# Halving normalized tokens before they are turned, turning them by DMA, and unrolling the experts of an attention and mixture-of-experts layer

## The reference

```python
x = L0_attn_x                                   # (2, 2048, 256) f32: 4096 tokens
xn = _layernorm(x, axis=-1)
scores = jnp.einsum('bqe,bke->bqk', xn @ W_qk, xn) * SCALE + (kpos - qpos) * alibi_slope[0]
attn = jax.nn.softmax(jnp.where(causal, scores, -jnp.inf), axis=-1)
s = jnp.einsum('bqk,bkd->bqd', attn, xn @ W_v.T)
...
probs = softmax(xf @ Wr); eidx = argmax(probs)  # 8 experts
rank = rank of the token in its expert; keep = rank < cap   # cap = 4096 / 8 = 512
xe = xf[dispatch]                               # (8, 512, 256)
h = jnp.maximum(jnp.einsum('ecd,edf->ecf', xe, W1), 0.0)    # F = 1024
ye = jnp.einsum('ecf,efd->ecd', h, W2) * (p_tok * valid)
return x + s * _silu(y)
```

## Time and profile before

| | us |
|---|---|
| median of 3 runs | 550.78 |
| lowest, highest | 549.56, 554.32 |
| the profiled execution's own time | 552.7 |
| its span | 551.0 |

### The profile page before, as it was taken

One profiled execution on the slowest core, in us unless ns is written; L12 is line 12 of the kernel. 1 busy time (PEld: TensorE's weight loads), 2 busy tenths in 40 slices (PEclk: granted clock), 3 DMA queues, 4 the chain that ended last, 5 costly groups with the idle time before them and its releaser, 6 DMA issues.

```text
span 551.0 us, 9415 instructions
## 1 busy us (share of the span) xinstructions
PE 464.2 (84%) x3222; PEld 320.9 (58%) x3222; DVE 365.5 (66%) x961; ACT 266.0 (48%) x559; POOL 218.5 (40%) x338
## 2 busy tenths in 40 slices
PE   4449798889999998999999999697969696979950
PEld 2135476557677765767667766464646464656630
DVE  3565798486577787867656549595968576865421
ACT  1223444253555444454444648474747465666620
POOL 4034836034105643630400020736464645546562
PEclk9788999979999999999999999898989899999985
DMA  2985230410230185040011270737363735432131
GB/s 77 300 300 189 82 113 29 121 53 2 75 117 2 47 278 175 2 151 4 28 45 8 79 250 22 227 92 228 88 219 95 209 106 150 150 80 75 39 92 41
DMA packets 36628, 61.20 MB, mean 111 GB/s; under 512 B 4230, under 2 KB 30476, under 8 KB 34544
## 3 DMA queue, kind: packets, MB, share of 16 engines
q1 hardware_dynamic: 30432, 43.47, 25.6%
q0 software_dynamic: 5632, 16.73, 9.6%
q10 hardware_dynamic: 528, 0.52, 0.3%
HBM read 35.46 MB, written 25.44 MB: 111 GB/s over the span
## 4 chain that ended last, share of the span: by engine, by line
PE 48%; DMA 19%; DVE 16%; issue 6%; ACT 6%; POOL 3%; SPq 1%; POOLq 0%; ACTq 0%; DVEq 0%
PE bank L1004 14%; PE bank L1006 13%; PE bank L1005 13%; DMA xe<-slots 8%; DMA tops<-wmax 5%; PE bank L1074 5%; DMA slots<-empty 4%; DVE pmax L745 2%; DVE pT_l L727 2%; ACT sc L905 2%; PE bank L1099 2%; DVE sc L714 2%; DVE so L739 1%; ACT pT_h L911 1%; ACT w_h L917 1%
## 5 line engine op out<-in xcount | busy, mean ns | idle before, releaser
L778 DVE TENSOR_TENSOR hid_l<-hid,hid_h 128x512 f16<-128x512 f32 x64 | 48.2, 753 | 58.5 <-ACT hid_h L932 58.0
L911 ACT ACTIVATE pT_h<-bank 128x512 f16<-128x512 f32 (+2 forms) x80 | 42.1, 529 | 83.6 <-PE bank L1074 83.4
L727 DVE TENSOR_TENSOR pT_l<-bank,pT_h 128x512 f16<-128x512 f32 (+2 forms) x80 | 48.6, 608 | 39.7 <-ACT pT_h L911 38.2
L1004 PE MATMUL bank<-v_h,pT_h 128*128 128x256 f16 x272 | 74.3, 273 | 0.2 <-DVE pT_l L727 0.2
L1005 PE MATMUL bank<-v_l,pT_h 128*128 128x256 f16 x272 | 74.3, 273 | 0.0
L1006 PE MATMUL bank<-v_h,pT_l 128*128 128x256 f16 x272 | 74.3, 273 | 0.0
L1004 PE MATMUL bank<-w_h,hid_h 128*128 128x256 f16 x256 | 73.2, 286 | 0.1
L1005 PE MATMUL bank<-w_l,hid_h 128*128 128x256 f16 x256 | 73.1, 286 | 0.0
L1006 PE MATMUL bank<-w_h,hid_l 128*128 128x256 f16 x256 | 73.0, 285 | 0.0
L905 ACT ACTIVATE sc<-sc,nbias 128x512 f32<-128x512 f32 (+2 forms) x80 | 51.8, 649 | 38.2 <-DVE nbias L720 37.8
L930 ACT ACTIVATE hid<-bank 128x512 f32<-128x512 f32 x64 | 38.2, 596 | 54.1 <-PE bank L1006 53.2
(11 more groups left out here) (149 smaller groups left out, 976.9 us busy)
## 6 DMA issues: line engine op xcount, KB each, us to landing
raw<-in_w_e SPq DMA_DIRECT2D x5, 2048.0 KB, 11.3
sc<-in_w_e SPq DMA_DIRECT2D x3, 2048.0 KB, 11.5
slots<-empty SPq DMA_DIRECT2D x1, 4224.0 KB, 19.6
xe<-slots SPq DMA_DIRECT2D x8, 528.0 KB, 6.2
out<-xg SPq DMA_DIRECT2D x8, 512.0 KB, 5.2
rows<-xg SPq DMA_DIRECT2D x8, 512.0 KB, 5.8
rows<-so SPq DMA_DIRECT2D x8, 512.0 KB, 3.2
xg<-in_x SPq DMA_DIRECT2D x7, 512.0 KB, 3.6
```

Source lines behind the costliest of these rows:

```text
L727: v.tensor_tensor(pT_l[:, t % 2, cols], tr_ps[n % 2][:, 0:w], pT_h[:, t % 2, cols], ALU.subtract).then_inc(pT_lo, 1)
L778: v.tensor_tensor(hid_l[:, f % HB, :], hid[:, f % 2, :], hid_h[:, f % HB, :], ALU.subtract).then_inc(h_lo, 1)
L911: a_.activation(pT_h[:, t % 2, c * GTOK:c * GTOK + w], tr_ps[n % 2][:, 0:w], ACT.Copy).then_inc(pT_hi, 1)
L1004: pe.matmul(ps, a_h, b_h, start=first, stop=False, skip_group_check=shared)
```

## The change

- The normalized group goes to a buffer of its own, `xn` (single), in f32. `split(g)`: ACT writes the high half and DVE the low half of the whole group, 128 x 1024 elements each, side by side into `xnr`, still one token per partition. The row that is scattered to `slots` is now the two f16 halves (512 x f16 in the place of 256 x f32) and the eight columns.
- `turn(g)`: SP issues four DMA transposes per group, one for each tile (128 tokens x 512 f16), from `xnr` into `xT`. The XT units of PE, ACT and DVE are gone, and QRY waits for all four transfers of its group (`xT_in`). `split(g)` for group `g` stands at the end of the last tile of group `g - 2`, one tile ahead of QRY(`g`).
- Experts: `next_rows` is now a DMA transpose of the expert's 512 rows in `slots` (512 x 512 f16) into `xeT`, and a small DMA of the eight columns (`enote`); both have two buffers. `turn_rows`, `turn_high`, `turn_low` are gone. The rows of experts 0 and 1 are fetched at tile 29.
- The hardware loops over the experts are unrolled on all engines.
- SP's queue is written in another order: it follows the tiles. At the start, `turn(0)` stands ahead of `slots<-empty`, and `turn(1)` ahead of the first expert weights.
- DVE does `normed(1)` and `split(1)` ahead of the first value unit; before, `normed(1)` stood behind the second.

```diff
@@ names and buffers @@
-HALVED = 8
-XT, QRY, VAL = 0, KD, 2 * KD
+HALVED = 6
+SPLIT, QRY, VAL = -1, 0, KD
...
+        xn = sb("xn", [P, GT, D])
         xnr = [sb(f"xnr{k}", [P, GT, ROW]) for k in range(2)]
+        halves = [xnr[k][:, :, 0:D].bitcast(F16) for k in range(2)]
...
-        xT_h = sb("xT_h", [P, KD, NG + 1, GTOK], F16)
-        xT_l = sb("xT_l", [P, KD, NG + 1, GTOK], F16)
+        xT = sb("xT", [P, NG + 1, GT, 2 * KD, P], F16)
...
-        xe = sb("xe", [P, SJ, ROW])
-        xeT_h = [sb(f"xeT_h{k}", [P, KD, CAP], F16) for k in range(2)]
-        xeT_l = [sb(f"xeT_l{k}", [P, KD, CAP], F16) for k in range(2)]
+        xeT = [sb(f"xeT{k}", [P, 2 * KD, CAP], F16) for k in range(2)]
+        enote = [sb(f"enote{k}", [P, SJ, ROW - D]) for k in range(2)]
@@ units_after @@
             if j == 0:
-                mine = [XT, XT + 1] * first + [QRY, QRY + 1] * last
+                mine = [QRY, QRY + 1] * last
             else:
                 mine = [[VAL, VAL + 1], [VAL + 2, VAL + 3], [RANK]][j - 1] * first
-            return late + [(g, n) for n in mine]
+            later = [(g + 1, SPLIT)] * (j == GT - 1 and last and g + 1 < GROUPS)
+            return late + [(g, n) for n in mine] + later
@@ SP @@
+            def turn(g):
+                at = key_slot(g // NG, g % NG)
+                if g > NG:
+                    sp.wait_ge(score_full, chunk_no(NT, 0))
+                sp.wait_ge(xn_lo, g + 1)
+                for j in range(GT):
+                    sp.dma_start_transpose(xT[:, at, j, :, :], halves[g % 2][:, j, :]).then_inc(xT_in[g % 2], 16)
...
+            def next_rows(e):
+                k = e % 2
+                if e >= 2:
+                    sp.wait_ge(h_full, (e - 1) * NF)
+                    sp.wait_ge(idx_made, e - 1)
+                sp.dma_start(enote[k][:, :, :], slots_e[e][:, :, D:ROW]).then_inc(enote_in[k], 16)
+                sp.dma_start_transpose(xeT[k][:, :, :], slots_r[e]).then_inc(xeT_in[k], 16)
...
+            turn(0)
+            sp.wait_ge(consts_made, 1)
+            sp.dma_start(slots.rearrange("(k p) r -> p k r", p=P),
+                         empty[:, :].unsqueeze(1).to_broadcast([P, T // P, ROW])).then_inc(slots_empty, 16)
+            group_out(0)
+            turn(1)
+            group_in(0)
+            sp.dma_start(raw[:, :, :], w_k[0]).then_inc(w_in[1], 16)
+            for t in range(TILES):
+                g = t // GT
+                if t % GT == 0 and g + 1 < GROUPS:
+                    group_out(g + 1)
+                if t % GT == 1:
+                    if g + 3 < GROUPS:
+                        group_in(g + 1)
+                    if g:
+                        group_s(g - 1)
+                if t % GT == GT - 1 and g + 2 < GROUPS:
+                    turn(g + 2)
+                if t == FIRST_SCALE - 1:
                     spread(0)
...
+            for e in range(E - 2):
+                spread(e + 2)
+                next_rows(e + 2)
+                if e + 3 < E:
+                    next_weights(e + 3)
@@ DVE (ACT's split makes xn_h in the same way, with scale X_UP) @@
+            def split(g):
+                k = g % 2
+                dve.wait_ge(xn_hi, g + 1)
+                if g >= 2:
+                    dve.wait_ge(slots_out[k], g // 2 * GT * 16)
+                    dve.wait_ge(xT_in[k], g // 2 * GT * 16)
+                v.scalar_tensor_tensor(xn_l[k], xn[:, :, :], X_UP, xn_h[k], ALU.mult, ALU.subtract).then_inc(xn_lo, 1)
@@ PE @@
-                    if more and f in TURN_AT:
-                        d = TURN_AT.index(f)
-                        pe.wait_ge(xe_lo, e * KD + d + 1)
-                        turn_rows(e + 1, d)
...
                     if n == QRY:
-                        pe.wait_ge(aux_read, u)
+                        pe.wait_ge(xT_in[g % 2], (g // 2 + 1) * GT * 16)
```

More of the change, by code:

```diff
@@ L221, in layer_kernel @@
         w_in = [sem("w_in_sc"), sem("w_in_raw")]
-        xe_in = sem("xe_in")
+        xT_in = [sem(f"xT_in{k}") for k in range(2)]
+        xeT_in = [sem(f"xeT_in{k}") for k in range(2)]
+        enote_in = [sem(f"enote_in{k}") for k in range(2)]
         back_in = [sem(f"back_in{j}") for j in range(SJ)]
@@ L433, in _ @@
             settle()
[L434 removed]
+            g_.memset(empty[:, D + TCOL:D + TCOL + 1], NOWHERE).then_inc(consts_made, 1)
             step(g_.memset(ident[:, :], 0.0))
@@ L565, in expert @@
                     fetch(e + 1, 1 - k, j)
-            with pool.Fori(0, E // 2 - 1) as i:
-                for k in range(2):
-                    expert(i * 2 + k, k)
-            expert(E - 2, 0)
+            for e in range(E - 1):
+                expert(e, e % 2)
             for j in range(SJ):
@@ L664, in unit @@
             def unit(g, n):
+                if n == SPLIT:
+                    split(g)
+                    return
                 u = g * UNITS + n
@@ L825, in _ @@
                 if t == FIRST_ROWS:
-                    for d in range(KD):
-                        turn_low(0, 0, d)
-                    dve.wait_ge(w_scaled, 1)
                     take_rows(0)
@@ L832, in _, with expert @@
             hidden(1, 1)
-            first_steps = count[0]
-            def expert(i, k, more, far, at):
-                e, o = i * 2 + k, 1 - k
+            def expert(e):
+                k, o, more, far = e % 2, 1 - e % 2, e + 1 < E, e + 2 < E
                 for f in range(NF):
@@ L943, in small_highs @@
                                   ).then_inc(small_hi, 1)
+            split(0)
+            small_highs()
             for n in range(RANK):
                 unit(0, n)
-                if n == XT + 1:
-                    small_highs()
+                if n == QRY + 1:
+                    split(1)
                 if n == VAL:
@@ L964, in _ @@
                     split_high(raw, 0, 0, q)
-                if t == FIRST_ROWS:
-                    for d in range(KD):
-                        turn_high(0, 0, d)
             act.wait_ge(consts_made, 1)
@@ L972, in _, with expert @@
                 hidden(f, f, True)
-            def expert(i, k, more):
-                e, o = i * 2 + k, 1 - k
+            def expert(e):
+                k, o, more = e % 2, 1 - e % 2, e + 1 < E
                 for f in range(NF):
@@ L991, in expert @@
                     a_.activation(gate[:, j, :], y_ps[k][j], ACT.Silu, scale=pk[k][:, j:j + 1]).then_inc(gate_made, 1)
-            with act.Fori(0, E // 2 - 1) as i:
-                for k in range(2):
-                    expert(i, k, True)
-            expert(E // 2 - 1, 0, True)
-            expert(E // 2 - 1, 1, False)
+            for e in range(E):
+                expert(e)
         @block.tensor
@@ L1010, in unit @@
                 a, at = aux[u % 2], key_slot(g // NG, g % NG)
+                if n == SPLIT:
+                    return
                 if u >= 2:
                     pe.wait_ge(aux_read, u - 1)
-                if n < QRY:
-                    if n == 0:
-                        pe.wait_ge(xn_made, g + 1)
-                    for j in range(GT):
-                        last = pe.transpose(a[:, j * P:(j + 1) * P], xnr[g % 2][:, j, n * P:(n + 1) * P], ident[:, :])
-                elif n < VAL:
+                if n < VAL:
                     if n == QRY:
-                        pe.wait_ge(aux_read, u)
+                        pe.wait_ge(xT_in[g % 2], (g // 2 + 1) * GT * 16)
                         if g == 0:
@@ L1092, in values @@
                     last.then_inc(pv_full, 1)
-            def turn_rows(e, d):
-                if d == 0:
-                    pe.wait_ge(xe_in, e * 16 + 16)
-                for j in range(SJ):
-                    last = pe.transpose(aux[d][:, j * P:(j + 1) * P], xe[:, j, d * P:(d + 1) * P], ident[:, :])
-                last.then_inc(xe_turned, 1)
             def up(e, f, k, first=False):
@@ L1194, in expert @@
                             down(e, f, k, range(j, j + 2))
-            with pe.Fori(0, E // 2 - 1) as i:
-                for k in range(2):
-                    expert(i, k, True)
-            expert(E // 2 - 1, 0, True)
-            expert(E // 2 - 1, 1, False)
+            for e in range(E):
+                expert(e)
 def kernel(**inputs):
```

218 lines of the change are left out of this document (94 added, 124 removed).

## The result

The changed kernel took 568.57 us (median of four runs, 564.75 to 570.45), the kernel before 550.37 (four runs beside it, 549.56 to 554.32). The ratio is 1.031, 95% interval 1.023 to 1.038: slower, by 18 us. The forecast was 553.5 in a range of 534 to 580, with 545 to 562 as the likeliest case. The profiled execution took 568.53 us with a span of 566.7. Executions fall into a faster and a slower state, and every ratio here is formed from the faster ones alone.

What follows compares the result with a forecast made beforehand. PE bounds the attention (busy 95%); in the experts PE waits for `xe`, with the weights' ring next. 552.7 + 4.4 + 14 - 15.7 = 555.4 for the profiled execution, 1.9 above the median, so 553.5 us; range 534 to 580.

Steps and rivals of the forecast that it cites:

- The experts, -15.7: Expert loop: removed turning and waits for `xe`, less new waits for weights, save 15.7 us in all.
- The ring of the weights' maxima: Experts: maxima out, weights issued, landed, DVE's reductions, maxima out; next limit, 26.3 us an expert instead of 28.2.
- The five intervals: Experts, from maxima to maxima: 26.3 us instead of 28.2, five times, -9.4 us, bounds -23.3 and +16.5.
- the first and the last expert: Ends of the expert loop: -3 us for the first (-1 to -4), -3.3 for the last (0 to -5).
- The attention, +14: Group boundaries: QRY waits for four transposes and moves by T less the cover; +14 us, bounds +9 and +37.
- T: Attention: time from a group's low half to its last transpose's landing; taken as 5.7 us, bounds 4.7 and 9.7.
- the cover: Attention: time from low half to the earlier QRY start, which hides part of T; 1.6 to 5.3 us by boundary.
- The start, +4.4: First groups: `slots<-empty` issued behind split(0) and four transposes, landing 2.5 us later; QRY of group 1 later; bounds -1, +12.
- C: Rival, slower: a transpose holds SP over 1.2 us, T passes 7.4; 570 us; decides from T = 6.2; chance 0.27.
- A: The forecast itself: two large terms, experts and attention, that cancel; 545 to 562 us; chance 0.42.
- B: Rival, faster: transposes no dearer than plain copies, T = 4.7, POOL's 23.5 us the experts' pace; 531 us; chance 0.25.
- D: Rival, much slower: 128 x 128 blocks turned one after another, T = 19.6; near 750 us; chance 0.06.

Runs made afterwards that it cites:

- x3: Changed kernel with the weights of expert e + 3 issued ahead of the rows of expert e + 2 in SP's queue; 561.37 us, ratio 1.033.
- x9: Changed kernel with QRY a tile later, weights issued before rows, POOL's wait at the first scatter, and the split a tile earlier; 535.00 us, ratio 0.974.
- x5: Changed kernel with dummy matmuls ahead of PE's wait for `xT` in groups 2 to 7; 561.87 us, ratio 1.034.
- x6: Changed kernel with POOL's wait for `slots<-empty` moved to just before the first scatter; 558.80 us, ratio 1.031.
- x2: Changed kernel with one DMA transpose a group instead of four, and four more small scatters a group on POOL; 563.97 us, ratio 1.038.

## Why the prediction was right or wrong

**The experts, -15.7: right.** The first pair of traces and the second both give -15.5. The ring of the weights' maxima was the next limit, as said: 26.1 us against 26.3, with DVE waiting 2.0 us for the weights on average (forecast some 3); with the weights issued first (x3) an expert takes 24.9. In the expert shown: maxima to issue of the weights 8.8 us (forecast 5.7; the transpose holds SP 2.3 to 4.4, not 1.2), issue to DVE's start 8.9 (forecast 11.3), DVE 8.8 (forecast 9.3). Two terms missed by 3.1 and 2.4 in opposite directions; the sum was luckier than its parts. The five intervals gave -10.3 (forecast -9.4), the first and the last expert -5.2 (forecast -6.3).

**The attention, +14: wrong in size; this is the step that failed.** It measured +25.4. The mechanism, T less the cover at each boundary, was right, and x9 shows it. The mis-sized term is T, "I take 5.7". It was 6.4 to 7.7, inside the bounds of 4.7 and 9.7. Within it the failed term is the "0.7 for each of three further issues": each came 1.3 us behind the one before. The 3.6 for one landing was about right (QRY starts 2.6 to 3.8 behind the last issue). The prediction had said that no row shows how long a transpose holds SP, and still took its price from plain issues; a transpose held the queue three times as long. The cover was read a little long as well: by the same reading groups 3 and 7 have 1.9 us, not 2.2 and 2.3. From QRY to QRY in the first pair of traces, each less the shift that it inherited:

| group | forecast | measured |
|---|---|---|
| 2 | +4.0 | +5.6 |
| 3 and 4 (4.8 us of stall absorbed) | +0.4 | +1.7 |
| 5 | +2.0 | +2.8 |
| 6 | +4.1 | +8.7 |
| 7 | +3.4 | +6.5 |

The longer T accounts for some 7 of the 11.4 missing. For the rest the forecast had no term. It stands in the rows of groups 6 and 7, 2.6 and 1.9 us beyond T, and next to nothing is left in that of group 5. PE's clock fits this: a row begins with the QRY matmuls of the group before it, and those of groups 5 and 6 took 2.3 and 1.9 us longer at the lower level, while those of group 4 kept the upper one. x5's trace agrees (its row 6 is 2.8 us shorter), its median does not, so the clock's share stays argued. Group 3's shift did vanish in the stall in the main: 4.8 us of it were absorbed, but with the longer T and the slow matmuls it was more than 4.8.

**The start, +4.4: measured +5.4.** The landing was forecast at 34.2 (34.3 measured), and normalizing and splitting took 3.7 us, as forecast. From the low half at 40.16 to QRY of group 1 it was 6.7 us, not 5.7. In that stretch PE has no wait for `xT`: it stood 11.2 us for the logits, which DVE reads behind its split, and then did the value units until 46.84, with 1.3 us of further waits, while the transposes' hold on SP ended at 45.48 and elsewhere QRY could start 1.3 us or more after that. So the value units, said to "fit in T", took all of it, and the trace does not say which of the two ended last. x6 takes the common wait away, and then the transposes are last (PE stands 3.5 us for them).

**The rivals.** What happened is C: 568.6 where it had 570. SP held 1.27 us for each transpose (C: over 1.2), T 7.0 on average (7.4), boundaries 25.4 (+23), start +5.4 (+6), experts -15.5 (-10). It had 0.27, the forecast 0.42. I gave the value of T by the nearest row in the trace, and C decided from T = 6.2, half a microsecond above my value, with most of the span between the bounds of 4.7 and 9.7 beyond it: the margin did not carry a higher chance for A than for C. B needed T at 4.7 and fell with it. D is refuted: 16 blocks in one transpose hold SP 1.3 to 3.6 us in x2, and T is 4.4 to 5.5 there, where D had 19.6. That the total of 568.6 lies in the range of 534 to 580 is owed to the width of the range: the value was 15 us too low. The Trainium skill, VectorE: DVE Perf Modes, section The three transpose paths, gives 1309 ns for one 128 x 128 transpose by DMA. Multiplied by the number of blocks, as for D (21 us), it does not agree with x2's trace, where sixteen blocks were turned and used 4.4 to 5.5 us after the low half. No run here has a transpose of a single block.

## What to carry to other kernels

Ask first how much of a gain needs the new mechanism: the earlier request for the rows was worth 17 us by itself, and the DMA transposes and the later fill of `slots` that came with it cost 30 in the attention, until both ends of the transposes' window were moved by a tile and POOL's wait was moved too. An operation with no row in the trace should not get the price of its plain relative; where the verdict turns half a microsecond above the chosen value, say that the verdict is open. A second buffer paid here only when the request also moved ahead of what it stood behind in its queue.

## What the runs showed of the hardware

In the changed kernel a DMA transpose of 128 x 512 f16 held SP's queue 1.19 to 1.38 us; one of 128 x 2048 held it 1.3 to 3.6 (x2), while the plain issue of `xe` held it 0.38. The hold was longer with much in flight: 8.6 us instead of 5.1 for four while a 4 MB fill ran (x6), 10.2 instead of 3.3 for one right behind 2 MB of weights (x3). That is no matter of transposes alone: the plain `out<-xg` right behind the fill held SP 7.9 us, and in the kernel before `raw<-in_w_e` right behind it 12.4, so the "at most 1.17" for a plain issue in the prediction holds for `xe` only. The kernel before ran in 550.4 us beside the first changed kernel and in 542.9 to 545.8 on the four chips afterwards, the changed one in 568.6 and 563.2, so a ratio needs both kernels measured side by side on one chip.
